# Perceiver layer on one core: batch 0's last head pairs first, and the experts batch by batch

## What is computed

```python
# 1 cross attention: 16 heads of 64, queries from x, keys and values from a context of 4096 tokens per batch
scores = einsum('bhqd,bhkd->bhqk', q, k) / 8;  x = x + (softmax(scores) @ v) @ w_o
# 2 self attention: 16 heads of 16, weights from a hyperbolic distance of q and k
dist = arccosh(max(1 + 2 * |q - k|^2 / max((1 - |q|^2) * (1 - |k|^2), 1e-6), 1))
x = x + (softmax(-dist) @ v) @ wo.T
# 3 experts: 8 of them, a token takes the one of its largest gate
h = gelu(xf @ W1[e] + b1[e]);  y = h @ W2[e] + b2[e];  x = x + y[argmax(softmax(xf @ Wg + bg))]
```

## Time and profile before

| | us |
|---|---|
| median of 3 runs (lowest, highest) | 1128.47 (1127.83, 1129.9) |
| the profiled execution | 1129.34 |
| its span, from the first to the last instruction | 1127.6 |

### The profile page before, as it was taken

The page is one execution under the profiler, slowest core; times in us unless marked ns, Lnnn a source line. Parts: engine busy times, 40 slices in busy tenths (PEclk is TensorE's granted clock), DMA queues, the critical chain, the costliest instruction groups (busy, mean ns, idle before and its releaser), DMA issues.

```text
span 1127.6 us, 36402 instructions
## 1 busy us (share of the span) xinstructions
PE 1050.3 (93%) x15389; PEld 784.1 (70%) x15389; DVE 795.9 (71%) x1034; ACT 789.5 (70%) x1416; POOL 674.5 (60%) x598
## 2 busy tenths in 40 slices
PE   5899999999999999999999999999999989755698
PEld 3477777777777777777777777777777776632355
DVE  4887777777777777777777777777677567565322
ACT  4776677777777777777777777777777766689643
POOL 3665666666666666666666666667766445346023
PEclk9999999999999999999999999999999989866899
DMA  9100000000000000000000000000030020000000
GB/s 328 50 2 16 7 17 7 17 7 16 7 17 6 17 8 16 7 16 8 16 7 17 8 16 7 16 12 2 7 114 8 2 76 2 2 1 1 1 1 19
DMA packets 27380, 25.43 MB, mean 23 GB/s; under 512 B 1850, under 2 KB 25938, under 8 KB 27218
## 3 DMA queue, kind: packets, MB, share of 16 engines
q1 hardware_dynamic: 27218, 23.10, 6.5%
HBM read 22.57 MB, written 0.52 MB: 20 GB/s over the span
## 4 chain that ended last, share of the span: by engine, by line
PE 78%; POOL 6%; issue 6%; ACT 5%; DVE 4%; DMA 1%; SPq 0%; POOLq 0%; DVEq 0%; ACTq 0%
PE ps L1245 15%; PE ps L1216 14%; PE ps L1321 13%; PE ps L1272 6%; PE ps L1365 5%; PE ps L1360 5%; PE ps L1363 5%; PE ps L1309 4%; POOL psums L1908 4%; PE ps L686 2%; PE ps L704 2%; PE ps L1300 1%; PE ps L1202 1%; PE ps L1174 1%; DVE m_part L1711 1%
## 5 line engine op out<-in xcount | busy, mean ns | idle before, releaser
L1908 POOL TENSOR_TENSOR psums<-probs 128x512 f16<-128x512 f32 x512 | 587.3, 1168 | 318.1 <-ACT probs L1551 262.5
L1542 ACT ACTIVATE probs<-ps 128x512 f32<-128x512 f32 x512 | 279.7, 600 | 208.6 <-PE ps L1321 208.2
L1711 DVE TENSOR_REDUCE m_part<-ps 128x2 f32<-128x1024 f32 x256 | 313.2, 1224 | 143.1 <-PE ps L1272 143.0
L1551 ACT ACTIVATE probs<-probs 128x512 f16<-128x512 f32 x384 | 242.6, 632 | 0.3
L1321 PE MATMUL ps<-q_hi,k_p 64*128 64x256 f16 x2048 | 211.9, 270 | 0.0
L1360 PE MATMUL ps<-v_sb,probs 128*128 128x65 f16 x2048 | 204.6, 192 | 1.7 <-POOL psums L1908 1.7
L1363 PE MATMUL ps<-v_sb,probs 128*128 128x64 f16 x2048 | 204.5, 192 | 0.0
L1365 PE MATMUL ps<-v_sb,psums 128*128 128x65 f16 x2048 | 204.1, 194 | 0.0
L1360 PEld LDWEIGHTS ps<-v_sb,probs 128*128 128x128 f16 x2048 | 188.4, 98 | 14.5 <-POOL psums L1908 1.9
L1363 PEld LDWEIGHTS ps<-v_sb,probs 128*128 128x128 f16 x2048 | 187.9, 97 | 14.8
L1365 PEld LDWEIGHTS ps<-v_sb,psums 128*128 128x128 f16 x2048 | 188.0, 97 | 0.0
(11 more groups left out here) (244 smaller groups left out, 1667.5 us busy)
## 6 DMA issues: line engine op xcount, KB each, us to landing
ctx_hi<-in_L_ffn_W_dram SPq DMA_DIRECT2D x2, 2048.0 KB, 10.0
wqk_raw<-in_L_xattn_w_q_dram SPq DMA_DIRECT2D x16, 128.0 KB, 2.2
wqk_raw<-in_L_xattn_w_k_dram SPq DMA_DIRECT2D x16, 128.0 KB, 2.7
probs<-in_ctx_dram SPq DMA_DIRECT2D x4, 512.0 KB, 7.0
wv_raw<-in_L_xattn_w_v_dram SPq DMA_DIRECT2D x16, 128.0 KB, 2.4
k_p<-in_ctx_dram SPq DMA_DIRECT2D x4, 512.0 KB, 9.2
wo_raw<-in_L_xattn_w_o_dram SPq DMA_DIRECT2D x16, 128.0 KB, 2.0
ctx_hi<-in_ctx_dram SPq DMA_DIRECT2D x7, 256.0 KB, 7.0
```

The costliest lines, as they stand in the source:

```text
L1542: nc.scalar.activation(p_raw[:, s:s + 2, h, :], ps[:, score_bank(n, pair, h), :].rearrange("p (k q) -> p k q", k=2), ACT.Exp, scale=XSCALE ...
L1551: nc.scalar.activation(p_hi[:, s % NP, :, :], p_raw[:, s % NX, :, :], ACT.Copy) \
L1711: nc.vector.tensor_reduce(m_part[:, j, t, :], ps[:, bank:bank + 2, :], AX.X, ALU.max) \
L1908: nc.gpsimd.tensor_tensor(p_lo[:, s % NP, :, :].rearrange("p h q -> p (h q)"), p_raw[:, s % NX, :, :].rearrange("p h q -> p (h q)"), p_hi[ ...
```

## The change

Three things change. ORDER lets batch 0's last three head pairs (5, 6 and 7) run as steps 10 to 12 and batch 1's as steps 13 to 15; DONE0 becomes 13. So the turning of the weights and batch 0's norm move from step 14 to step 13; the projections, squares and lengths of batch 0's row groups, and the splits of W1, move from step 15 to step 14, one row group in each period; inverses, placing and units stand earlier in step 15, and so do the splits of W2. The value projections of step 15 are gathered in its first pairs. The two roots of group 0 go to the front of ACT's tail, and some tiles lie elsewhere.

The experts are computed batch by batch: 32 chunks of 256 columns. Batch 0's gates and norm come as soon as its self attention is added, and the last steps of batch 1's self attention (turning and projecting the output, norm, gates) are put between the chunks of batch 0. The copies of turned tiles move from ACT to DVE. The root of the variance of batch 0's last norm is taken as exp(0.5 ln) among the logarithms and exponentials; batch 1's remains a square root, at chunk 7, and its gate exponentials stand at chunk 14.

```diff
-ORDER = tuple((i // 2, i % 2) for i in range(STEPS - 4)) + tuple(
-    (hp, b) for b in range(B) for hp in (HP - 2, HP - 1))
-DONE0 = STEPS - 2
+ORDER = tuple((i // 2, i % 2) for i in range(STEPS - 6)) + tuple(
+    (hp, b) for b in range(B) for hp in range(HP - 3, HP))
+DONE0 = STEPS - 3
...
-OUT_AT, NORM_AT, OT_AT, Y_AT = 4, 5, 7, 12
+OUT_AT, NORM_AT, OT_AT, Y_AT = 4, 5, 6, 9
...
-INVERSES_AT = {9: (0, 1, 2, 3), 10: (4, 5, 6, 7), 11: (8, 9, 10)}
-PLACED_AT = {16: (0, 1), 17: (2, 3)}
-UNIT_AT = {18: (0,), 19: (1,), 20: (2, 3), 21: (4,), 22: (5,), 23: (6,), 24: (7,), 25: (8,), 26: (9,),
-           27: (10,), 28: (11, 12), 29: (13,), 30: (14,), 31: (15,)}
-HIGH_AT = {1: 0, 3: 1, 5: 2, 7: 3, 28: 4, 29: 5, 30: 6, 31: 7}
-LOW_AT = {1: 0, 3: 1, 5: 2, 7: 3}
+W1_IN = {0: 0, 2: 1, 4: 2, 6: 3}
+VALUES_AT = {0: (1, (0,)), 1: (1, (1,)), 2: (2, (0, 1)), 3: (3, (0, 1)), 4: (4, (0, 1)), 6: (5, (0, 1)),
+             8: (6, (0, 1)), 10: (7, (0, 1))}
+INVERSES_AT = {1: (0, 1, 2, 3), 2: (4, 5, 6, 7), 3: (8, 9, 10)}
...
+PLACED_AT = {6: 0, 7: 1, 8: 2, 9: 3}
+UNIT_AT = {10 + u: u for u in range(16)}
+HIGH_AT = {22: 4, 24: 5, 26: 6, 28: 7}
+LOW_AT = {23: 4, 25: 5, 27: 6, 29: 7}
...
+HIDDEN_BANK, MASK_BANK = 1, 3
+LAST = E * NC
+TURN_OUT_AT, PROJECT_AT, TURN_XN_AT, LOGITS_AT = 3, 5, 10, 13
+RESIDUAL_AT, NORMAL_AT, PARTS_AT, GATES_AT = 6, 9, 11, 14
...
+            def hidden(k):
+                b, i = divmod(k, LAST)
+                e, it = divmod(i, NC)
+                if i == 0:
+                    pe.wait_ge(s_xl, b + 1)
+                if k >= 2:
+                    pe.wait_ge(s_hg, k - 1)
+                n = 0
+                for c in range(NC):
+                    for w_part, x_part in ((0, 0), (0, 1), (1, 0)):
+                        mm = pe.matmul(ps[:, HIDDEN_BANK + k % 2, 0:TQ],
+                                       w1_p[:, w_part, e, c, it * P:(it + 1) * P],
+                                       xnT_p[:, x_part, c, b * TQ:(b + 1) * TQ], start=(n == 0), stop=(n == 5))
+                        n += 1
+                mm.then_inc(s_h, 1)
...
+            def mask(k):
+
+                b, i = divmod(k, LAST)
+                if i == 0:
+                    pe.wait_ge(s_bc, 1 + 2 * (b + 1))
+                pe.wait_ge(s_hm, k)
+                pe.matmul(ps[:, MASK_BANK, 0:TQ], sel_b[:, i // NC, :], best_b[:, b * TQ:(b + 1) * TQ],
+                          start=True, stop=True).then_inc(s_mk, 1)
...
+            def outer(k):
+                b, i = divmod(k, LAST)
+                e, it = divmod(i, NC)
+                pe.wait_ge(s_hl, k + 1)
+                for t in range(2):
+                    for h_part, w_part in ((0, 0), (0, 1), (1, 0)):
+                        mm = pe.matmul(ps[:, SUM_BANKS[b], t * D:(t + 1) * D],
+                                       hid_p[:, k % 4, h_part, t * P:(t + 1) * P],
+                                       w2_p[:, w_part, e, it, :], start=False,
+                                       stop=(i == LAST - 1 and h_part == 1), skip_group_check=True)
+                mm.then_inc(s_yo, 1)
...
             turn_output(0)
             project_output(0)
             turn_normalised(0)
+            average(4, 1, 0)
             logits(0)
+            average(5, 1, 1)
+            turn_average(4, 1, 0)
+            average(6, 1, 2)
+            turn_average(5, 1, 1)
             pe.wait_ge(s_el, 8)
             hidden(0)
             hidden(1)
+            average(7, 1, 3)
+            turn_average(6, 1, 2)
+            turn_average(7, 1, 3)
+            for k in range(B * LAST + 2):
+                if 2 <= k < B * LAST:
+                    hidden(k)
+                    if k % NC == 0 and k % LAST:
+                        mask(k)
+                if k >= 2:
+                    outer(k - 2)
+                if k % LAST == 1 and k < B * LAST:
+                    turn_best(k // LAST)
+                    mask(k - 1)
+                    biases(k // LAST)
+                if k == TURN_OUT_AT:
+                    turn_output(1)
+                if k == PROJECT_AT:
+                    project_output(1)
+                if k == TURN_XN_AT:
+                    turn_normalised(1)
+                if k == LOGITS_AT:
+                    logits(1)
...
+            roots(0)
             act.wait_ge(s_vone, 2)
             take_turned_output()
+            root_of_product(1)
             root_of_variance(act, 2, slice(2, NT))
+            root_of_sum(1)
             take_values(0)
             take_batch(act, 1)
             for i in range(9):
                 take_rows(act, i, 1)
+                if i in (1, 3):
+                    root_of_product(2 + i // 2)
+                if i in (2, 4):
+                    root_of_sum(1 + i // 2)
+                if i >= 7:
+                    logarithms(i - 7)
...
+            for gg in range(4, 7):
                 logarithms(gg)
+            act.wait_ge(s_ln, LN * 3 + 3)
+            nc.scalar.activation(rstd[:, 0:2], var[:, 0:2], ACT.Ln).then_inc(s_lv, 1)
+            logarithms(7)
+            act.wait_ge(s_lv, 1)
+            nc.scalar.activation(rstd[:, 0:2], rstd[:, 0:2], ACT.Exp, scale=0.5).then_inc(s_sd, 1)
             for gg in range(4, 8):
                 weights(gg)
+
+            def gates(b):
+                act.wait_ge(s_g, 10 * b + 2)
+                nc.scalar.activation(ge[:, 2 * b:2 * b + 2, :], lg[:, 2 * b:2 * b + 2, :], ACT.Exp) \
+                    .then_inc(s_ge, 1)
...
+            gates(0)
+            for k in range(B * LAST + 1):
+                if k < B * LAST:
+                    act.wait_ge(s_h, k + 1)
+                    if k == 0:
+                        act.wait_ge(s_bc, 1)
+                    if k >= 2:
+                        act.wait_ge(s_hm, k - 1)
+                    nc.scalar.activation(hid[:, k % 2, :], ps[:, HIDDEN_BANK + k % 2, 0:TQ], ACT.Gelu,
+                                         bias=b1_T[:, k % LAST:k % LAST + 1], scale=1.0 / ES) \
+                        .then_inc(s_hg, 1)
+                if k % LAST == 1:
+                    take_best(k // LAST)
+                if k >= 1:
+                    act.wait_ge(s_hm, k)
+                    if k >= 5:
+                        act.wait_ge(s_yo, k - 4)
+                    nc.scalar.activation(hid_p[:, (k - 1) % 4, 0, :], hid_m[:, (k - 1) % 2, :],
                                          ACT.Copy).then_inc(s_hh, 1)
+                if k == RESIDUAL_AT + 1:
+                    root_of_variance(act, 4, slice(2, NT))
+                if k == GATES_AT:
+                    gates(1)
...
+            def masked(k):
+                dve.wait_ge(s_hg, k + 1)
+                if k % NC == 0:
+                    dve.wait_ge(s_mk, k // NC + 1)
+                if k >= 2:
+                    dve.wait_ge(s_hl, k - 1)
+                nc.vector.tensor_tensor(hid_m[:, k % 2, :], hid[:, k % 2, :], ps[:, MASK_BANK, 0:TQ],
+                                        ALU.mult).then_inc(s_hm, 1)
...
+            take_average(4)
+            shifted_logits(0)
+            take_average(5)
+            take_average(6)
+            first_best(0)
+            take_average(7)
             normalise(1)
+            for k in range(B * LAST):
+                if k == TURN_OUT_AT + 1:
+                    take_turned(3, 1, OUT_BANKS[1][0])
+                if k == RESIDUAL_AT:
+                    residual(1)
+                    variance(4, slice(2, NT))
+                if k == NORMAL_AT:
+                    normalised(4, slice(2, NT))
+                if k == PARTS_AT:
+                    take_normalised(1)
+                if k == GATES_AT:
+                    shifted_logits(1)
+                if k == LAST:
+                    first_best(1)
+                if k == LAST + 4:
+                    add_experts(0)
+                masked(k)
+            add_experts(1)
...
+                    if n == DONE0 + 1:
+                        qk(pe, q, 0)
...
+                    if n == DONE0 + 1:
+                        lengths(pe, q, 0)
...
+                    if n == DONE0 + 1:
+                        if q in W1_IN:
+                            split_experts_high(act, W1_IN[q])
+                        squares(act, q, 0)
+                        rows(act, q, 0)
...
+                    if n == DONE0 + 1 and q >= 1:
+                        low_rows(dve, q - 1, 0)
...
-            for k in (6, 7):
-                split_experts_low(dve, k)
```

More of the change, by code:

```diff
@@ L445, in tail_pool @@
                 pool.wait_ge(s_r2, gg + 1)
-                if gg == 2:
-                    pool.wait_ge(s_iq, 2 * IQ)
-                nc.gpsimd.tensor_tensor(ratio[gg], root[:, gg % 2, :, :], ratio[gg], ALU.add) \
+                nc.gpsimd.tensor_tensor(ratio[gg], root_of(gg), ratio[gg], ALU.add) \
                     .then_inc(s_ra, 1)
-            for i in range(E * NC):
+            for i in range(B * LAST):
                 pool.wait_ge(s_hh, i + 1)
@@ new lines, in biases @@
+            def biases(b):
```

(45 more changed lines are left out.)

414 lines of the change are left out of this document (186 added, 228 removed).

## The result

| | before | after |
|---|---|---|
| median of 7 runs each, us | 1128.45 | 1133.91 |
| lowest, highest | 1124.47, 1129.9 | 1132.13, 1139.32 |
| profiled execution, its span | 1127.6 | 1131.4 |

The ratio is 1.0066, with a 95% interval from 1.0049 to 1.0083: 0.7% slower, where 0.9% faster was forecast. The windows by stage of the after, to be read against the earlier trace rows (stretch, its us, busy us of PE, PEld, DVE, ACT, POOL with their instructions, PEclk, DMA share, GB/s): steps 13, 14 and 15, the last 46 us up to the last weights, from there to the third hidden product, and from there to the last product.

A forecast was written before the change was run, and what follows sets the result against it. PE was taken to bound the steps and expert loop, ACT's chained functions the stretch between. Gains 4.4 + 22.1 less 16.0 and 0.1 made 10.4 us, off the median 1128.5 giving 1118.1 us; range 1107 to 1127.

The forecast's parts named there:

- the steps: Steps 13 to 15: 188.0 us in place of 192.4, 4.4 us less, with bounds of -1 to 9.
- a clock under 0.9 in the loop: Sign in the expert loop: a PE clock this low would make the prediction wrong.
- a step 14 above 71 us: Sign in step 14, forecast at 67.1 us: a longer time than this would make the prediction wrong.
- Steps 13 and 14: Step 13 takes 59.7 us with batch 0's turning and norm; step 14 takes 67.1 with its eight row groups.
- Step 15: Last attention step: 61.2 us in place of 77.3, losing 11.2 us of PE work and its two worst stalls.
- The last weights: ACT's tail after the steps: roots of batch 1 about 5 us earlier, 1.2 lost, so last weights end 3.9 us earlier.
- From the last weights to the third hidden product: Stage before the loop: 7.6 us in place of 25.8; third hidden product 22.1 us earlier, bounds 18 to 24.
- The loop: Expert loop: period 1.54 us per half chunk, plus 10.8 for batch 1's steps; 59.3 in place of 43.3, 16.0 given back.
- The clock rival: Expert loop: PE granted 1.2 GHz; gain gone from 9 or 10 of 32 chunks, 1154 us with all; chance 0.08.
- That the overlap isn't had: Expert start: GELU queues behind batch 1's last weights, so batch 0's experts can't start earlier; already in the sum, no chance given.
- The longer chain: Expert loop: POOL's fixed part, contention or batch 1's path stretch the period to 1.75; 1126 us; chance 0.16.
- PE pacing the loop: Expert loop: POOL and ACT finish early enough, period 1.41, and two steps have no stalls; 1111 us; chance 0.19.

The follow-up runs named there:

- the first experiment: The changed kernel's order of head pairs and steps, but the experts for all 512 tokens at once as before; 1128.65 us, ratio to before 1.0011.
- ACT's order: The changed kernel with ACT's tail queue reordered: logarithms 0 and 1 behind the row groups, then placed tiles, batch 0's variance logarithm behind batch 1's last; 1128.95 us, 1.0015.
- the fills: The changed kernel with 28 products of no use, outer products three chunks behind and ACT's queue reordered, plus 22 more such products in PE's waits; 1120.19 us, 0.9930.
- three mends: The changed kernel with 28 products of no use ahead of batch 0's turned norm, outer products three chunks behind and ACT's queue reordered; 1122.72 us, ratio to before 0.9970.
- all at once with fills: The changed kernel's order of head pairs with all experts at once, ACT's queue reordered and 67 products of no use in PE's waits; 1120.07 us, 0.9940.
- the after with 55 of them: The changed kernel, ACT's queue and two-chunk distance kept, with 55 products of no use in PE's waits; 1128.26 us, ratio to before 1.0017.
- the 28 products: The changed kernel with 28 extra products of 512 columns on PE, of no use, ahead of batch 0's turned norm; 1131.26 us, ratio to before 1.0036.

## Why the prediction was wrong

The mechanism of the split was seen rightly, and a sum of the right shape was added up from terms of which every one was too favourable. Two of the results lie outside the bounds that the prediction gave them: the steps cost 1.9 us (its bounds were -1 to 9 gained), and the third hidden product came 15.4 us earlier (18 to 24). Neither of the two signs that it named as making it wrong, a clock under 0.9 in the loop or a step 14 above 71 us, appeared.

**Steps 13 and 14** were right: 60.4 and 66.8 us for 59.7 and 67.1.

**Step 15** (61.2, measured 67.7; before took 77.9 cut at the same events, 77.3 in the earlier trace rows) is the largest miss. The step that failed is the sum of PE's work and waits in it. By PE's rows from 898.3 to 925.7, pairs 0 to 4 took 27.4 us where the working had 18.4 + 2 (its own items add up to 18.85). Left out were the last row group's products, which fall into this step (1.55), the turn and projection of step 14's output (1.4) and the placing of batch 0's inverse lengths (1.5). Counted too low were the P*V slots (thirteen, 5.0 us, for ten, 3.7) and the scores, of which a sixth set falls in (5.9 for 5.0); value tiles were counted too high (four, 5.6 us, for five, 6.65), the gathers right (3.55). Waits were 2.7 for 2. Pairs 5 to 12 took 27.8 for 30, which is partly luck: a cast on DVE takes about 1.25 us from start to start where 0.5 stood, and of the 3 us of hand-overs DVE waited 0.8. DVE is busy for 26.7 of these 27.8 us and PE for 27.3, so which of the two sets the pace isn't shown. The end took 12.5 for 10.8. One subtraction shows the slip: PE was busy 70.1 us in this step before and lost 11.2 by the forecast's own account, which leaves 58.9 us of work. 61.2 left 2.3 us for all waits, and the drain through POOL alone has 3.6. Measured were 59.9 busy and 7.8 idle.

**The last weights** (3.9 earlier, measured 1.2). Two terms failed. "1.2 are lost where the logarithm of batch 0's variance waits" was 2.9 by ACT's row. And the "about 5 us" (5.1) of the roots was 4.0, as the first experiment shows, where that variance isn't waited for.

**From the last weights to the third hidden product** (7.6, measured 11.6). The items were right: at a clock of 1.00 the same chain takes 7.4 (ACT's order) and 7.7 us (the fills), and in both, as in the after, the turn of batch 0's norm starts 5.3 us ahead of the end of the last weights. What failed is the clock that was assumed for it. The text named 1.2 GHz as the bound of this term (18 instead of 22.1) with the 0.63 of the earlier trace rows beside it, and then took the full clock: the nearest row spoke for the other end.

**The loop** (59.3, measured 61.5). The period was right, 1.54 forecast and 1.55 measured, with PE's wait for POOL in front of the outer group (of every second one; POOL's operation takes 0.67 us where 0.60 stood), and so were the table switches (two holes of 2.1, 3.8 us for both when taken away). What was missing are the clock (0.97 in this stretch; at 1.00, with the fills, it is 60.2) and about a microsecond spread over the steps of batch 1. The clock rival was thus at work, but in the profiled run at a tenth of its price: 1.3 us where it put 10 for the gain to be gone; the change needed no ten chunks at 1.2 GHz to fail, since the sum was off elsewhere. What was held against this rival was a misreading: the gaps of 0.2 to 0.4 us in the loop before are those of the weight load, while PE itself stood still for 0.6 of 39.0 us. In the after PE stands still for 6.9 of 61.5.

**The comparison itself.** The 22.1 us were counted against a stage of before that itself ran at 0.80: at 1.00 it takes 22.5 us, not 25.8. Of the net 2.2 that the two expert terms left (18.2 less 16.0), nothing stands once both versions have the same clock and ACT's order, and even that takes the outer products three chunks behind. The forecast sign hung on 4.4 + 3.9 us in the steps and the weights, and these were the least supported terms.

That the overlap isn't had was rightly turned down. The longer chain (1.75 a chunk) and PE pacing the loop (1.41) were not seen; with three chunks of distance the period is 1.47.

## What to carry to other kernels

Check a sum made of parts against the busy time of the same window less what is removed: what it leaves for waits has to cover at least the ones already seen. Work that is moved out of a serial tail into a busy loop is not hidden there, and every function that the loop doesn't use adds a table switch (3.8 us for two here); with the costlier half chunks, 14.8 us saved came back as 14.4. And where PE has short bursts between ACT's tiles, price its work at the clock shown there, or fill the waits before judging the restructuring.

## What was not expected of the hardware

The runs of one kernel differ by their granted clock, and their time follows it. Of the after's seven runs, four had a mean of 0.968 or 0.969 and took 1132.1 to 1133.9 us, three had 0.961 or 0.962 and took 1137.5 to 1139.3. The kernel with its three mends and fills had 0.979 to 0.982 in six runs and stayed within 1.5 us, all at once with fills within 1.2. Fills alone don't bring this: the after with 55 of them had 0.973 to 0.980 in twelve runs and spread over 8.3 us. A part of the spread arises where all versions have the same code: over the 14 traces the first sums are copied out between 115.7 and 120.0 us, and in the three latest (119.3 to 120.0) the clock was 0.96 both in the first 40 us and from 80 to 120.

A full clock in one stage did not carry over to the next. In the run with ACT's order alone the stage before the loop was at 1.00 and the loop at 0.90; with the 28 products it was at 0.79 and the loop at 0.97. The same loop code took 61.5, 64.0, 65.6 and 67.0 us at 0.97, 0.92, 0.90 and 0.87, so its own waits don't settle its clock alone. In the split version both stages stayed at 1.00 only with PE's waits filled in both; with all experts at once the loop ran at 1.00 without any, before and with ACT's order. The Trainium skill (TensorE: Matmul & The Clock Gate, A second HAM failure mode: psum-queue depth-cycling) ties such swings to short idles between groups that cycle through PSUM banks. The traces agree as far as the idles go: with the same banks and the waits filled, the clock holds at 1.00. No run here changes the banks alone.

22 products of no use (some 4.7 us of PE, by the 6.21 that 28 of them take) took 2.5 us off the median of the kernel with the three mends, and 4.5 by the ratios to before on each chip. The fastest two versions here, 1120.1 and 1120.2 us, are 0.6 to 0.7% faster than before.
